# A megakernel of attention and a routed feed-forward part: new numbers and new picking rules in the planner that sets the order of all instructions

## The reference

```
xn  = layernorm(x)
out = x + attention(xn) + ffn(xn)

attention: q, k, v = xn Wq', xn Wk', xn Wv'; 16 heads of 16; q and k rotated (RoPE)
           softmax(causal(q k' / 4)) v, then Wo'
ffn:       m = mixk[0]*xn[t-1] + mixk[1]*xn[t] + mixk[2]*xn[t+1]
           nine paths (m W1[p] + b1[p]) W2[p] + b2[p]; the row takes the path
           argmax(tanh(m Wo1 + bo1) Wo2 + bo2)
           layernorm(xn + path) * gamma + beta
```

## Time and profile before

| | us |
|---|---|
| three runs, median | 817.83 |
| lowest, highest | 816.98, 821.49 |
| the profiled execution | 820.42 |
| its span, first to last instruction | 818.1 |
| PE busy, share | 765.1, 94% |
| DVE busy, share | 657.5, 80% |
| ACT busy, share | 451.0, 55% |
| POOL busy, share | 289.9, 35% |

### The profile page before, as it was taken

How to read it: one execution, slowest core, us unless ns; L and a number is a source line. 1 busy time by engine, 2 the same in 40 slices (tenths; PEclk the granted TensorE clock), 3 DMA queues, 4 the chain that set the end, 5 groups by cost and what they waited for, 6 DMA issues and landing times.

```text
span 818.1 us, 12610 instructions
## 1 busy us (share of the span) xinstructions
PE 765.1 (94%) x4416; PEld 363.7 (44%) x4416; DVE 657.5 (80%) x1894; ACT 451.0 (55%) x780; POOL 289.9 (35%) x459
## 2 busy tenths in 40 slices
PE   4769998999999999899999999899999999999996
PEld 2423334344455433345455443335355553354434
DVE  5988799788798788888988788888988878877722
ACT  2362543765556653775466654476556665654672
POOL 1001022891335122593244313387161502030622
PEclk9965899999999999999999999999999999999999
DMA  6368041213612524022550715022550515100013
GB/s 232 107 169 162 1 89 22 68 62 85 127 28 40 116 83 78 30 79 73 106 82 2 155 54 107 1 69 78 117 104 2 107 50 103 25 13 2 6 22 77
DMA packets 40576, 59.96 MB, mean 73 GB/s; under 512 B 4813, under 2 KB 36830, under 8 KB 37634
## 3 DMA queue, kind: packets, MB, share of 16 engines
q1 hardware_dynamic: 36002, 54.39, 28.1%
q0 software_dynamic: 4224, 4.19, 3.4%
q10 hardware_dynamic: 288, 0.59, 0.2%
HBM read 42.04 MB, written 16.85 MB: 72 GB/s over the span
## 4 chain that ended last, share of the span: by engine, by line
PE 81%; DVE 11%; ACT 3%; DMA 2%; POOL 1%; issue 1%; SPq 0%; POOLq 0%; ACTq 0%; DVEq 0%
PE bank L1548 16%; PE bank L1510 15%; PE bank L1529 15%; PE bank L1501 9%; PE bank L1491 7%; PE bank L1453 5%; PE bank L1576 3%; PE bank L1464 3%; PE bank L1471 2%; ACT prob L1123 2%; DVE bank L1341 2%; PE bank L1558 2%; DVE piecemax L1344 1%; PE bank L1519 1%; PE bank L1478 1%
## 5 line engine op out<-in xcount | busy, mean ns | idle before, releaser
L1123 ACT ACTIVATE prob<-bank 128x512 f32<-128x512 f32 x576 | 326.1, 596 | 249.8 <-PE bank L1529 245.4
L1341 DVE CUSTOM_DVE_ANT_0 bank<-bank,causal_sb 128x384 f32<-128x384 f32 (+3 forms) x512 | 241.2, 510 | 48.3 <-PE bank L1510 46.5
L1510 PE MATMUL bank<-k_st,q_st 96*128 96x512 bf16 (+3 forms) x768 | 239.3, 341 | 8.4 <-DMA q_st<-scratch 4.5
L1005 POOL TENSOR_SCALAR_AFFINE_SELECT prob<-prob 128x256 f32<-128x256 f32 (+1 forms) x320 | 132.7, 456 | 263.1 <-ACT prob L1123 260.0
L1529 PE MATMUL bank<-q_st,k_st 98*128 98x512 bf16 (+3 forms) x768 | 216.6, 335 | 7.1 <-ACT prob L1123 3.2
L1344 DVE TENSOR_REDUCE piecemax<-bank 128x1 f32<-128x512 f32 x256 | 166.0, 683 | 28.9 <-PE bank L1510 28.4
L1548 PE MATMUL bank<-prob,v_sb 128*17 128x512 f32 (+3 forms) x1536 | 159.6, 502 | 0.1
L1510 PEld LDWEIGHTS bank<-k_st,q_st 96*128 96x128 bf16 x768 | 72.1, 99 | 145.7 <-DVE piecemax L1341 36.4
L1529 PEld LDWEIGHTS bank<-q_st,k_st 98*128 98x128 bf16 x768 | 71.0, 99 | 113.9 <-ACT prob L1123 53.8
L1501 PE MATMUL bank<-w_sb,mid 128*128 128x256 f32 (+1 forms) x320 | 85.3, 388 | 0.4 <-DVE z L1332 0.3
L1453 PE MATMUL bank<-xnT,wqk_sb 128*128 128x512 f32 x128 | 68.1, 637 | 6.1 <-ACT xnT L1070 4.4
(11 more groups left out here) (82 smaller groups left out, 693.4 us busy)
## 6 DMA issues: line engine op xcount, KB each, us to landing
scratch<-parts SPq DMA_DIRECT2D x16, 768.0 KB, 3.8
q_st<-scratch SPq DMA_DIRECT2D x90, 128.0 KB, 6.9
k_st<-scratch SPq DMA_DIRECT2D x15, 384.0 KB, 4.7
z<-in_x SPq DMA_DIRECT2D x8, 512.0 KB, 4.1
mask<-chosen SPq DMA_DIRECT2D x16, 256.0 KB
z<-in_x POOLq DMA_DIRECT2D x8, 512.0 KB, 6.2
out<-z SPq DMA_DIRECT2D x8, 512.0 KB, 4.3
k_st<-scratch SPq DMA_DIRECT2D x15, 256.0 KB, 5.4
```

The source lines that it names most:

```text
L1005: nc.gpsimd.affine_select(out=d, in_=d, compare_op=ALU.is_ge, fill=0.0, base=0, pattern=pattern, channel_multiplier=-1).then_inc(masked, 1)
L1123: nc.scalar.activation(prob[:, place_of(G, i), :], ps[:, :], ACT.Exp, scale=float(DK) ** -0.5).then_inc(act_took, 1)
L1341: nc.vector.tensor_tensor_reduce(ps, ps, causal_sb[:, HALF - w:HALF], 1.0, NEG, ALU.add, ALU.max, to).then_inc(dve_took, 1)
L1510: nc.tensor.matmul(begin(("max", G, u))[:, 0:w], q_st[0:PARTS, G % STACKS, h, t * P:(t + 1) * P], k_st[0:PARTS, G % STACKS, h, k0:k0 + w], ...
```

## The change

The kernel's instructions, their shapes, the semaphores, the banks and the nominal times of `plan()` stay as they are. What changes is the table and the picking in `arrange()`:

- Nearly every cost of VectorE, ScalarE and GpSimd is lowered, and `SIGNAL` is raised from 0.12 to 0.20. (`LATE` moves all later line numbers up by two and the new lines in `arrange()` by four more: line 1510 of before is line 1516 of the changed kernel.)
- `STALL` goes from 8 to 20: a foreseen wait of 1 us now outweighs 0.4 of a group of nominal time, where it was 0.16. `WINDOW` goes from 0.3 to 0.4.
- DMAs other than `place` are put into the list 1.5 us later than their inputs are ready (`LATE`).
- An item of VectorE, ScalarE or GpSimd that isn't ready yet holds back younger items of the same engine, unless these would be done before it could start (`soon`).
- Where no TensorE item is possible, the next other item is the one that can start first.

```diff
--- before.py
+++ after.py
@@ -488,13 +488,13 @@
 
 PE_US = {"xnT": 0.44, "qk": 0.86, "v": 0.86, "early": 0.86, "mid": 0.86, "paths": 0.86, "proj": 0.86, "scores": 1.0,
          "onehot": 0.45, "S": 0.22, "shift": 0.25, "oT": 0.44, "attnT": 0.44}
-OWN_US = {"stats": 2.7, "norm": 2.7, "rest": 1.54, "lo": 1.34, "mix": 1.3, "last": 1.15, "root": 1.4, "cut": 0.9,
-          "hi": 1.04, "mid_cut": 1.04, "osum": 0.6, "ynorm": 0.6, "pow": 1.1, "turn": 1.27, "rope": 1.27, "sel": 0.5,
-          "scale": 1.27, "affine": 1.27, "addx": 1.3}
-DMA_US = {"load": 5.0, "store": 3.5, "fill": 9.0, "keep": 2.5, "spread": 5.0, "place": 2.4, "out": 4.0, "addx": 5.0}
-TAKE_US = {"S": 0.6, "shift": 0.57, "v": 0.59, "early": 1.37, "scores": 1.7, "onehot": 0.67, "mid": 0.75,
-           "paths": 0.69, "oT": 0.85, "proj": 0.69, "xnT": 0.65, "attnT": 0.65, "qk": 0.59}
-SIGNAL = 0.12
+OWN_US = {"stats": 2.1, "norm": 2.2, "rest": 1.2, "lo": 1.15, "mix": 1.1, "last": 1.05, "root": 1.1, "cut": 0.6,
+          "hi": 0.95, "mid_cut": 0.95, "osum": 0.48, "ynorm": 0.49, "pow": 1.0, "turn": 1.23, "rope": 1.22, "sel": 0.33,
+          "scale": 1.23, "affine": 1.23, "addx": 0.9}
+DMA_US = {"load": 4.5, "store": 4.0, "fill": 7.0, "keep": 2.5, "spread": 5.0, "place": 2.4, "out": 4.0, "addx": 5.0}
+TAKE_US = {"S": 0.5, "shift": 0.48, "v": 0.5, "early": 1.3, "scores": 1.6, "onehot": 0.6, "mid": 0.67,
+           "paths": 0.61, "oT": 0.72, "proj": 0.61, "xnT": 0.55, "attnT": 0.55, "qk": 0.5}
+SIGNAL = 0.2
 
 
 def engine_of(name):
@@ -515,19 +515,21 @@
 
 def take_us(name):
     if name[0] == "max":
-        return 0.17 + MAX_UNITS[name[2]][4] * 0.00106 if has_diagonal(name[2]) else 0.69
+        return 0.11 + MAX_UNITS[name[2]][4] * 0.00101 if has_diagonal(name[2]) else 0.6
     if name[0] == "qk" and name[1] == 0:
-        return 1.4
+        return 1.2
     return TAKE_US[name[0]]
 
 
 
 NARROW = ("pv", "shift", "scores", "onehot")
 CHANGE = 0.11
-WINDOW = 0.3
+WINDOW = 0.4
 BACKLOG = {"dve": 0.4, "act": 0.8, "pool": 1.5, "dma": 100}
+
+LATE = 1.5
 GROUP_US = 50
-STALL = 8
+STALL = 20
 
 
 def arrange(items):
@@ -623,17 +625,21 @@
                 if best is None or key < best[0]:
                     best = (key, met, n)
             else:
-                others.append((met, e, n))
-        now = max(free["pe"], best[1]) if best else 1e9
-        go = None
+                others.append((met + (LATE if e == "dma" and name[0] != "place" else 0), e, n))
+        now = max(free["pe"], best[1]) if best else free["pe"]
+        go, soon = None, {}
         for met, e, n in others:
             late = pending[0][0] >= pending[n][0] - 0.02
+            start = max(met, free[e])
+            if e in soon and start + OWN_US[pending[n][1][0]] > soon[e] + SIGNAL:
+                continue
             if met <= max(free[e], now) and (free[e] <= now + BACKLOG[e] or late and free[e] <= now + 2 * BACKLOG[e]):
                 go = n
                 break
+            if e in ("dve", "act", "pool"):
+                soon[e] = min(soon.get(e, start), start)
         if go is None and best is None:
-            assert others, pending[:5]
-            go = min(others)[2]
+            go = min(others, key=lambda x: (max(x[0], free[x[1]]), x[2]))[2]
         emit(*pending.pop(best[2] if go is None else go))
     return out
```

## The result

The changed kernel takes 786.57 us (median of 4 runs, 784.53 to 789.22), the kernel before 817.92 us on the same chip (4 runs): a ratio of 0.9602, 95% interval 0.9557 to 0.9646. The forecast was 800 us, the range 787 to 814. The profiled execution took 784.53 us, its span is 782.5 us, so 35.6 us of span are gone.

The account below looks back on a forecast made before the run. TensorE was taken to set the pace, VectorE close behind. Terms 9.0 + 7.5 + 1.5 + 4.0 - 4.0 = 18.0 us, from the profiled 820.4 to 802.4, less 2.6 for the median: 800 us, range 787 to 814.

Parts of the forecast that it names:

- the first 62 us and the slow clock of the stretch behind them: Start of the kernel: order as given and slow clock (0.59) behind it stay, so no gain was counted there.
- part 5: VectorE's table: truer durations, but no margin for GpSimd's holds; new waits take 4 us off the gain (0 to 26).
- Part 1: TensorE's whole order: 45 fewer runs of narrow matmuls at 0.20 us each save 9.0 us (4.1 to 9.9).
- Part 2: Turn between images: `norm` and one `cut` move clear of GpSimd, `xnT` and `shift` waits shrink, 7.5 us (-2 to 10.3).
- Parts 3 and 4: `S` waits less for `place`'s DMAs, 1.5 us; banks 6 and 7 are reused less tightly, 4 us.
- Part 4: Banks 6 and 7: 17 instead of 34 reuses stand close behind the previous matmul, saving 4 us (0 to 8).
- Rival 2: More gain: a fifth of the hidden 52.1 us of `S` load waits goes through STALL, 10 us more: 790 us; chance 0.14.
- Rival 1: Given back: runs merge (9 us), but avoided waits reappear at the next item as VectorE is nearly full: 809 us; chance 0.18.
- Rival 3: Slower: without margin, GpSimd holds 24 of 30 VectorE items and TensorE pays 26 us: 822 us; chance 0.08.
- rival 4: No change: the gain from merged runs falls into waits TensorE has anyway: 816 us; chance 0.08.

Follow-up runs that it names:

- `warm_b`: The kernel before plus eleven unused float32 matmuls of 512 columns in TensorE's pauses before 62 us: 813.49 us against 822.64, ratio 0.9872.
- `stall8`: The changed kernel with STALL put back from 20 to 8, all else new: 808.07 us, ratio 0.9832 to the kernel before.
- run 6: Not a follow-up run: the words "a run 6 to 9" mean 0.14 to 0.20 us per merged run of narrow matmuls, 6 to 9 us in all.
- `norm_late`: The changed kernel with `norm` and the last two `xnT` of images 1 to 3 put back to about their old places: 792.53 us against 786.47.
- `norm_early`: The kernel before with the second half's `norm` moved 19 to 23 items earlier in images 1 to 3: 819.46 us against 822.64.
- `t_table`: The kernel before with the new durations alone, old STALL, WINDOW and picking rules kept: 804.29 us, ratio 0.9786.
- `margin`: The changed kernel with larger costs for `rest`, `lo`, `norm` and `cut`, as margin for GpSimd's holds: 806.72 us, ratio 0.9841 to the kernel before.
- `short_b`: The kernel before with GpSimd's rotation cut to 64 columns instead of 256 per half, order untouched: 807.76 us against 822.64.
- `short_a`: The changed kernel with GpSimd's rotation cut to 64 columns instead of 256 per half, order untouched: 781.67 us, ratio 0.9493 to the kernel before.
- `b_stall20`: The kernel before with STALL raised from 8 to 20 and nothing else changed: 811.7 us against 818.75, ratio 0.9912.

## Why the prediction was wrong, step by step

**Two steps failed**; of the 13.4 us that the forecast lacks the first is worth some 5, the second 4 and more. The first is the sentence that the first 62 us and the slow clock of the stretch behind them stay. It priced the clock at nothing. The first 62 us did stay (gaps 19.5 and 19.7 us), but the clock did not: over the executions on one chip its mean was 0.966 before and 0.974 after, worth some 5 us by the line of the 48 executions, and the table's 13.7 us come from a profile whose clock, 0.980, none of the changed kernel's ten executions exceeds. That the clock can be moved without touching the order is shown by `warm_b`. That the new order moves it by having fewer pauses is argued, not shown, and in the stretch that I had named it need not move at all: 0.59 before, 0.82 in one profile of the changed kernel, 0.59 in the other.

The second is part 5, which took 4 us off for the missing margin, and with it the sum's 18 us for the order itself. At equal clock the changed kernel gains some 27 us, 9 of them in the start, where my terms held 2 by even shares and nearer 4 by the single waits (2.0, 1.3 and three runs). Without part 5's term the forecast would have been 796, with 5 us for the clock besides 791; the rest lies in the runs, 12 us instead of 9.0, and in what I can't part.

**Part 1, runs** held in mechanism and nearly in size. The entry to a run still costs 0.09 us, 0.31 from start to start where two matmuls of 512 columns have 0.22, as in the earlier trace rows:

```profile
222.63 0.38 PE L1535 MATMUL bank<-q_st,k_st 98*128 98x512 bf16 x1
222.94 1.49 PE L1554 MATMUL bank<-prob,v_sb 128*17 128x384 f32 x24
```

The merged runs' exits are 7.7 us by the matmul starts; with 45 entries of 0.09 to 0.10 in the gaps it makes some 12, just above my upper end of 9.9, and by `stall8`'s 0.14 to 0.20 a run 6 to 9. I had taken 9.0.

**Part 2, the turn** was under-sized, and its mechanism only half right. I had 7.5 us for three turns. The lead grows by about 7 us over each of the last two; the second image's, with 2.0 us of waiting at 137 us that is gone, is part of the start's 10.1. The waits that I had listed did go: `xnT` for `norm` and most of `shift` for `cut`. `norm_late` gives 6.1 us back when `norm` is put back, but through ScalarE's bank and the clock instead of a hold. Six `cut`s stayed beside a rotation, as I had counted, and all six were held for 1.20 us; the one at 313 us cost TensorE only 0.34 us, as it had other work meanwhile. The Trainium skill's rule that the one that starts first keeps the other out for its whole instruction (SBUF — State Buffer, section "Who interferes with whom") agrees with this trace by that 1.20 us; how often the loser is passed over it doesn't say, and the 6.15 us of `norm_early` show more than one instruction's worth.

**Parts 3 and 4** came out as said where they can be read: no wait on a DMA from 82 us on, and the gaps of `paths` fell by 2.5 us. Part 4 has no experiment of its own.

**Part 5, new waits**, had the wrong sign in the sum. The truer table alone gave 17.5 us (`t_table`), and putting the margin in cost 20 (`margin`), 12 of them at equal clock. Waits did appear, at `max` (7.7 us of gaps), but those at `S`, `shift`, `xnT`, `paths` and `pv` fell by 20 in all. By `short_b` and `short_a` the holds do not cost the changed kernel 4 us more than the kernel before; whether they cost it less is not resolved.

**Rival 2**, the hidden part of `S`'s waits, came true in part of its size, and not by its mechanism: `S`'s gaps fell by 6.5 us where I would have had 10, but by the second count they are 16.3 us before, 16.4 with `STALL` 20 alone (`b_stall20`), 11.5 with the new durations alone (`t_table`) and 10.1 in the changed kernel. So it is the durations that shrink them, and hardly the weight. That its 790 us lay nearest is luck. **Rival 1** wanted the maxima's load waits to grow by as much as the runs save. They grew by 34 us and the time fell all the same. That sign was badly chosen: a load's wait costs only what the matmul ahead doesn't cover, and only 7.7 of these 34 us show as gaps between matmuls. So the prediction was wrong too where it called the loads' rows an upper bound to read losses from. **Rival 3** fell with `short_a` and the result, **rival 4** with the result.

The range failed because its lower end came from the ends of the terms that I had, and the clock had none.

## What to carry to other kernels

A stretch that shows a low granted clock is not a fixed cost: give the clock a term with ends in the forecast of a reordering; a few unused matmuls in the pauses are a cheap trial of what it is worth. Before a gain is put down to the clock of one profile, set clock and span of all executions against each other: here the one profile said 13.7 us and the executions some 5. A list schedule's durations and its weight on waits gave 17.5 and 7 us alone and 31.4 with the picking rules, and the schedule reacts by 20 us to four numbers, so no item's number can be judged by that item's own rows. Price lost TensorE time by the distances between matmul starts; the load waits for one kind moved by 34 us the wrong way while the kernel got faster.

## What the runs showed of the hardware that was not expected

- A waiting VectorE instruction can be passed by several GpSimd instructions in a row: 6.15 us for a `rest` of some 1.2 us (`norm_early`), during three rotations of 1.25 us and four selections of some 0.40 us. I had reckoned with one hold of 1.1 us.
- The same program meets a different clock from one execution to the next: 30.8 and 44.4 us at the lower level, spans of 782.5 and 786.4 us. Over 48 executions of the kernel before, 0.001 of mean granted clock goes with 0.63 us of span.
- Eleven unused matmuls of 512 columns in pauses before 62 us raised the granted clock from 0.66 to 0.84 from 41 to 62 us and made the kernel 1.3% faster [0.8, 1.7].
